# First attention stage: order of the floor rows' turn, of key low parts in halves, and of loads of queries, values, weight pieces and x

## What is computed

```python
ifg = jnp.concatenate([q, k, v], axis=-1)          # q = layernorm(x), k = v = ctx
ig = (ifg @ igate_w.T + igate_b).T
fg = (ifg @ fgate_w.T + fgate_b).T
log_f = jax.nn.log_sigmoid(fg)
cs = jnp.cumsum(log_f, axis=1)
log_D = where(mask, cs[:, :, None] - cs[:, None, :], -inf) + ig[:, None, :]
max_log_D = jnp.max(log_D, axis=-1, keepdims=True)
D_mat = jnp.exp(log_D - max_log_D)
C = jnp.einsum('hsd,htd->hst', qh, kh) / np.sqrt(DH) * D_mat
normalizer = jnp.maximum(jnp.abs(C.sum(axis=-1, keepdims=True)), jnp.exp(-max_log_D))
h = jnp.einsum('hst,htd->hsd', C / (normalizer + EPS), vh)
x = x + (h - mu) / jnp.sqrt(var + LN_EPS) * ln_scale
```

## Time and profile before

| | |
|---|---|
| median of 3 runs | 562.37 us (560.95 to 563.0) |
| the profiled execution | 565.76 us |
| its span, first to last instruction | 564.0 us |
| mean granted TensorE clock | 0.992 |
| TensorE matmul busy | 542.1 us, 96% |
| TensorE weight load busy | 455.0 us, 81% |
| VectorE busy | 324.3 us, 58% |
| ScalarE busy | 236.1 us, 42% |
| GpSimd busy | 72.7 us, 13% |

### The profile page before, as it was taken

One profiled execution on the slowest core, in us unless ns is written; L12 is line 12 of the kernel. 1 busy time (PEld: TensorE's weight loads), 2 busy tenths in 40 slices (PEclk: granted clock), 3 DMA queues, 4 the chain that ended last, 5 costly groups with the idle time before them and its releaser, 6 DMA issues.

```text
span 564.0 us, 8422 instructions
## 1 busy us (share of the span) xinstructions
PE 542.1 (96%) x2773; PEld 455.0 (81%) x2773; DVE 324.3 (58%) x792; ACT 236.1 (42%) x440; POOL 72.7 (13%) x107
## 2 busy tenths in 40 slices
PE   6899898999999999899999999999999999999996
PEld 5687687888988888778888878889788889788886
DVE  6568879868777698763434552443543543633333
ACT  6435546648798742561122351122441122531111
POOL 6233424203311432000000000000000000000000
PEclk9999899999999999999999999999999999999999
DMA  6684616273959676100000100000000000000001
GB/s 178 186 230 116 179 46 203 56 257 123 403 193 281 247 241 213 46 1 1 0 1 0 38 2 1 0 1 19 20 0 1 1 1 29 9 1 0 1 0 40
DMA packets 29860, 47.44 MB, mean 84 GB/s; under 512 B 3392, under 2 KB 21184, under 8 KB 29440
## 3 DMA queue, kind: packets, MB, share of 16 engines
q1 hardware_dynamic: 24848, 30.14, 16.8%
q0 software_dynamic: 4848, 16.78, 9.2%
q10 hardware_dynamic: 128, 0.05, 0.0%
HBM read 40.27 MB, written 2.10 MB: 75 GB/s over the span
## 4 chain that ended last, share of the span: by engine, by line
PE 58%; issue 8%; POOL 2%; DVE 1%; POOLq 0%; ACT 0%; DVEq 0%; ACTq 0%
PE ps L942 57%; POOL rstd L453 1%; POOL h L564 1%; PE ps L598 0%; PE ps L906 0%; DVE qr L1577 0%; DVE x L1565 0%; DVE xn L1326 0%; DVE h L1624 0%; DVE alT L1604 0%; ACT silD L1272 0%; DVE xT L1333 0%; POOL w L553 0%; POOLq L564 0%; POOL w L555 0%
## 5 line engine op out<-in xcount | busy, mean ns | idle before, releaser
L1289 ACT ACTIVATE h<-ps,scol 128x512 f32<-128x512 f32 x64 | 44.1, 690 | 175.3 <-PE ps L942 175.2
L942 PE MATMUL ps<-hBt,h 128*128 128x512 f32 x512 | 117.5, 390 | 0.0
L942 PE MATMUL ps<-hA,h 128*128 128x512 f32 x512 | 117.3, 390 | 0.0
L942 PEld LDWEIGHTS ps<-hA,h 128*128 128x128 f32 x512 | 95.9, 188 | 20.4 <-DVE hA L1631 0.6
L942 PEld LDWEIGHTS ps<-hBt,h 128*128 128x128 f32 x512 | 95.8, 188 | 20.3 <-DVE hBt L1631 0.6
L942 PE MATMUL ps<-xT,w 128*128 128x512 f32 x256 | 61.8, 396 | 1.3 <-DVE xT L1333 1.0
L942 PEld LDWEIGHTS ps<-xT,w 128*128 128x128 f32 x256 | 46.4, 188 | 15.2 <-issue 5.9
L1649 DVE CAST hBt<-h 128x512 fp32r<-128x512 f32 x32 | 13.7, 427 | 73.7 <-ACT h L1289 73.7
L1649 DVE CAST hA<-h 128x512 fp32r<-128x512 f32 x32 | 13.7, 427 | 70.0 <-ACT h L1289 70.0
L453 POOL TENSOR_TENSOR rstd<-ve,mhalf 128x4 f32<-128x4 f32 x16 | 16.4, 1024 | 262.9 <-DVE ve L1321 262.9
L1272 ACT ACTIVATE silD<-ps,scol 128x512 f32<-128x512 f32 x32 | 22.0, 689 | 45.6 <-PE ps L942 45.6
(11 more groups left out here) (176 smaller groups left out, 885.0 us busy)
## 6 DMA issues: line engine op xcount, KB each, us to landing
looked<-w_all_in SPq DMA_DIRECT2D x16, 704.0 KB, 5.6
h<-w_all_in POOLq DMA_DIRECT2D x16, 512.0 KB, 6.8
V<-ctx_in SPq DMA_DIRECT2D x8, 512.0 KB, 4.5
Qb<-xT SPq DMA_DIRECT2D x64, 64.0 KB, 2.1
w<-w_all_in POOLq DMA_DIRECT2D x3, 1024.0 KB, 6.9
x<-x_in SPq DMA_DIRECT2D x4, 512.0 KB, 5.0
kstA<-ctxT_in SPq DMA_DIRECT2D x4, 512.0 KB, 4.7
kstC<-ctxT_in SPq DMA_DIRECT2D x4, 512.0 KB, 6.4
```

Source lines behind the costliest of these rows:

```text
L942: last = mm(o, a, b, start=(k == 0 and p == 0), stop=(k == n_k - 1 and p == 1))
L1289: fn(h32[:, m % 2, :], ps[:, 2 + m % 4, :], ACT.Gelu, scale=scol[:, L + 1, m:m + 1])\
```

## The change

- The loads of x of groups 3 and 4 are issued behind the startup constants instead of behind the first queries.
- In a group, SyncE issues the third sequence's queries, then the next keys, then the gate rows, then the last sequence's queries, and only then waits for the product with V and issues the next values, directly ahead of the z rows.
- The low part of the keys is made in two instructions of 512 columns with a counter for each; the gate matmuls wait for the first half and, one chunk later, for the second. The second attention keeps whole ones.
- GpSimd issues the weight pieces behind h_root of the first sequence and inv_root instead of ahead of them.
- TensorE turns the floor rows behind the last sequence's scores instead of before its exponents, and VectorE copies them behind the last two weighings instead of behind x's normalisation.

```diff
@@ sync
             sp.dma_start(diag[:, :], diag_in).then_inc(s["consts"], 16)
+            for g in range(2, G):
+                sp.dma_start(x[:, Q * g:Q * g + Q, :], x_in[Q * g:Q * g + Q].rearrange("b s d -> s b d"))\
+                    .then_inc(s["x_rest"], 16)
             sp.wait_ge(s["klo_done"], 1)
...
             queries_in(0, 0, 0)
-            for g in range(2, G):
-                sp.dma_start(x[:, Q * g:Q * g + Q, :], x_in[Q * g:Q * g + Q].rearrange("b s d -> s b d"))\
-                    .then_inc(s["x_rest"], 16)
...
+                    queries_in(g, u, 2)
                     with sp.If(i < 1):
 
                         sp.wait_ge(s["klo_done"], 2 + u)
                         sp.dma_start(kstA[:, :, :], ctxT_in[:, :, (2 + u) * GT:(3 + u) * GT])\
                             .then_inc(ctxT_ld[u], 16)
-                    queries_in(g, u, 2)
-                    def early():
+                    if u == 0:
                         gates_in(gn)
+                    else:
+                        with sp.If(i < 1):
+                            gates_in(gn)
+                    queries_in(g, u, 3)
+                    def following():
                         sp.wait_ge(s["pv_done"], Q * g + 2)
                         values(gn, 1 - u)
+                        lead_in(gn, 1 - u)
                     if u == 0:
-                        early()
+                        following()
                     else:
                         with sp.If(i < 1):
-                            early()
-                    queries_in(g, u, 3)
-                    if u == 0:
-                        lead_in(gn, 1 - u)
-                    else:
-                        with sp.If(i < 1):
-                            lead_in(gn, 1 - u)
+                            following()
@@ gpsimd
+            def k_lo_apart(n, u):
+
+                pool.wait_ge(s["khi_done"], n + 1)
+                for c, name in ((0, "klo_first"), (1, "klo_done")):
+                    nc.gpsimd.tensor_tensor(kT[:, u, 1, c, :], kstA[:, c, :], kT[:, u, 0, c, :], ALU.subtract)\
+                        .then_inc(s[name], 1)
...
                         with pool.If(i > 0):
-                            k_lo(G - 1, kstA[:, :, :], 1)
+                            k_lo_apart(G - 1, 1)
                             h_root(2 * Q - 1, 1)
                     else:
                         with pool.If(i < 1):
-                            k_lo(2, kstA[:, :, :], 0)
+                            k_lo_apart(2, 0)
                         h_root(Q * g - 1, 1)
+                    h_root(Q * g, 0)
+                    inv_root(g + 2)
                     if u == 0:
                         pool.wait_ge(s["gate_moved"], 32 * (g + 2))
                         pool.sem_inc(s["pieces_go"], 1)
...
                             pieces(1, 0)
-                    h_root(Q * g, 0)
-                    inv_root(g + 2)
@@ tensor
                     if c == KD:
+                        pe.wait_ge(s["klo_first"], g + 1)
+                    if c == KD + 1:
                         pe.wait_ge(s["klo_done"], g + 1)
...
-                        if q == Q - 1:
-                            more(lambda: turn_e(gn))
-                            if u == 1:
-                                if_later(pe, i, flag_total)
+                        if q == Q - 1 and u == 1:
+                            if_later(pe, i, flag_total)
                         for k in (2 * q, 2 * q + 1):
                             expo(g, u, k)
                         for k in (2 * q, 2 * q + 1):
                             qk(g, u, k)
+                        if q == Q - 1:
+                            more(lambda: turn_e(gn))
@@ vector
             def k_lo(n, par):
                 dve.wait_ge(s["khi_done"], n + 1)
-                v.tensor_tensor(kT[:, par, 1, :, :], kstA[:, :, :], kT[:, par, 0, :, :], ALU.subtract)\
-                    .then_inc(s["klo_done"], 1)
+                for c, name in ((0, "klo_first"), (1, "klo_done")):
+                    v.tensor_tensor(kT[:, par, 1, c, :], kstA[:, c, :], kT[:, par, 0, c, :], ALU.subtract)\
+                        .then_inc(s[name], 1)
...
                             x_norm(g + 2, (8, 12)[u] - 8 * i)
-                            more(lambda: floor_copy(gn, 1 - u))
                             head_norm(b - 2, q - 2)
                         if q == Q - 1:
+                            more(lambda: floor_copy(gn, 1 - u))
                             finish(b - 1, u, q - 1)
```

More of the change, by code:

```diff
@@ L235, in two_layers @@
             raw_here raw_seen hnm_ready hve_ready lns_ready gw_lo gw_cast const_set mv_ready rstd_ready xn_ready tr_done xhi_done xlo_done x_free
-            khi_done klo_done gate_done gate_copied gate_moved ab_ready ln_ready ncs_ready er_ready z_ready
+            khi_done klo_done klo_first gate_done gate_copied gate_moved ab_ready ln_ready ncs_ready er_ready z_ready
             z_moved er_turned et_ready expo_done d_ready qk_done c_ready pv_done pv_used hstat_ready hrs_ready
```

## The result

| | before | after |
|---|---|---|
| median | 562.2 us (560.09 to 566.24, 22 runs) | 566.35 us (563.13 to 570.3, 22 runs) |
| the profiled execution | 565.76 us | 565.2 us |
| its span | 564.0 us | 563.5 us |
| its mean granted TensorE clock | 0.992 | 0.997 |

The ratio of the times is 1.0057 with an interval of 1.0038 to 1.0077: the change makes the kernel 0.57% slower, some 3.2 us by this ratio (4.15 between the medians). The forecast was 2.4 us faster, and the range ended at 562.9.

What follows compares the result with a forecast made beforehand. TensorE was taken to bound the kernel, busy 322.8 of the last 328 us. Terms summed to -3.95 us, -2.35 with one clock fall, so 562.4 - 2.4 = 560.0 us; range 557.8 to 562.9.

Steps and rivals of the forecast that it cites:

- x sooner: At the start, z rows land at 24.6 us: 1.4 us gained, and 1.6 more if the clock holds.
- Turn of the floor rows: At each group's end, Er waits go and x's turn waits for VectorE's copy: +0.45, -1.6, +0.7 us in groups 1 to 3.
- Queries ahead of values: On SyncE's queue, the last sequence's queries land in 2.0 us instead of 4.5 to 4.8, but zero time is gained.
- Weight pieces later: Pieces beside the next group's z rows and first queries cost 0.3, 0 and 0.2 us in groups 1 to 3.
- upper bounds of 1.7, 0.4 and 1.7: Most that waits for the next group's first queries could cost beside the weight pieces, groups 1 to 3: 3.8 us in all.
- The rule of turns between queues: DMA engines go round robin between queues, so GpSimd's pieces slow SP's loads in any order: 3.8 us instead of 0.5.
- Halves: Key low parts in two instructions cut TensorE's wait from 0.63 to 0.1 us: 0.5 gained in groups 2 and 3 each.
- Clock falls: Idle time of some 2.0 us before x's turn in three groups halves the clock once, costing 1.6 us.
- (d): Rival, chance 0.07: slower, weight pieces delay first queries at the first score block of groups 2 to 4; 563.3 us at full price.

Runs made afterwards that it cites:

- pieces put back: The after kernel with GpSimd's weight pieces put back ahead of h_root and inv_root, everything else kept: 560.31 us, ratio 0.9941.
- `lows` later: The after kernel with GpSimd's subtraction `lows` moved behind the second sequence's h_root: 566.08 us, ratio 1.0023.
- copy put back: The after kernel with VectorE's floor copy put back behind x's normalisation, TensorE's turn of the floor rows left late: 566.9 us, ratio 1.0078.
- turn undone: The after kernel with floor copy and weight pieces put back, and TensorE's turn of the floor rows again ahead of the last exponents: 558.97 us, ratio 0.9894.
- both put back: The after kernel with both VectorE's floor copy and GpSimd's weight pieces put back where before had them: 558.08 us, ratio 0.9898.

## Why the prediction was wrong, step by step

*x sooner* (-1.4, -1.6): right. Forecast 24.6 for the first z matmul, found 24.20 after 0.34 us of waiting, and clock 1.00 at 26 to 28 us. The first product with V came 3.4 us sooner, against 3.0. Over the runs it brought only 1.9, by the version with x alone: the fall that it avoids is in the trace of before, but not in every execution (see the end of this section).

*Turn of the floor rows* (+0.45, -1.6, +0.7): its mechanism was right. No Er is left; in its place stands the wait before the turn of x, 2.74, 1.57 and 2.44 us where 2.0 were forecast, 2.05 and 2.05; VectorE shows no gap before its last two weighings. The 0.45 lost in group 1 is borne out where nothing else disturbs it: with the pieces put back x is turned 12.45 us behind the first product with V (31.07 to 43.52), and 11.95 in before (34.59 to 46.54). The excess of 0.9 and 0.65 in groups 1 and 3 is `x_norm` (2.29 and 2.03 for 1.38), and no term of the sum had it. I had costed what moves on GpSimd's queue by its issues and roots and not by `lows`, which is moved too and reads two inputs beside VectorE. The experiment with `lows` later shows the cause. The Trainium skill (SBUF — State Buffer, Who interferes with whom) says that VectorE and GpSimd share one pair of ports, and that a `tensor_scalar` may be of a kind that takes it, so that the second to come waits. The rows agree roughly in size: 0.9 us more beside a subtraction of 0.75, and 0.65 more beside one of 0.78.

*Queries ahead of values* ("zero for all of it"): wrong. The landing times came nearly as forecast (2.0 us for the last sequence's; 5.2, 3.1 and 4.8 for the next group's first, forecast 4 or more), but undoing this order costs 3.5 us. I read 0.66, 0.85 and 0 of waiting for queries in before and took them for the whole lateness. TensorE came to them late because of Er. The gain of the turn that I booked as -1.6 rests on this edit: without it the turn alone measures 1.0019, and turn and copy together 1.0075.

*Weight pieces later* (+0.3, 0, +0.2): this is the term that failed. With the pieces put back, the stretches from the first product with V to the first scores of groups 2, 3 and 4 take 14.29, 23.51 and 23.64 us. In after they take 16.68, 23.81 and 25.49: 4.5 us more in all, where 0.5 was booked, and some 6 over the runs. In these 4.5 are the longer `x_norm` (0.9 and 0.65) and the fall (1.4); in group 1 they leave hardly anything for the z rows and queries, which land while TensorE waits for the copy. The traffic by itself is seen in the version with `lows` later: 2.0, -0.3 and 1.95 us. That is the upper bounds of 1.7, 0.4 and 1.7, and a little above them in groups 1 and 3; I had chosen values near the lower ones. Where the copy is out of the way as well, the z rows alone are waited for by 2.44, 1.22 and 2.94 us (copy put back), against 1.50, 0 and 0 with the pieces put back too.

Three things in it were wrong. I reasoned from bytes (1.8 MB at 343 GB/s end at 48.3), as if it were enough that the bulk ends before the queries are wanted. The end itself was put too early: 48.3 is 44.9 in after, whose start is 3.4 us ahead, but the last piece, issued at 40.08, lands 6.3 us later, at 46.4, and 39.6 to 47.6 us carries 2.15 MB, the second sequence's queries with it. And the small transfers end with the bulk, not at their share: in copy put back the pieces issued at 39.16 and 39.70 land at 44.6 and 46.5, and the z row issued at 39.20 is waited for until 45.9. Last, I asked only when the first queries are wanted. The z rows are wanted before them (44.89 against 45.36 with the pieces put back), and in before they were issued ahead of the queries, at 41.0 to 43.6, just where the pieces' issues were put; in front of that TensorE was already waiting for the copy. The rule of turns between queues (the Trainium skill, DMA: Bandwidth & Descriptors, in its part on queues, rings and completion order) that I set beside the row, and then weighed lower than the bytes, is borne out by the 2.0 and 1.95 us.

*Halves* (-0.5, -0.5): the durations are right (2.53 for two, 1.27 each, forecast 1.28), the wait for low parts is gone, and the time is unmoved by it: 0.9897 against 0.9898. A gain of up to 0.5% is not excluded by the intervals.

*Clock falls*: one of three forecast, one in the trace, behind the longest idle time of 2.74 us, at 1.4 us by the first score (forecast 0 to 1.6). The idle times of 1.79, 1.57 and 1.79 us with the pieces put back showed none in the profiled execution, and the others' mean clocks (0.998 to 1.0) leave room for one short one at most. So the number in the profiled execution was right and the number over runs was not: after's mean clock is 0.994 (0.988 to 1.0), that of the 34 runs of before 0.996. The stretched `x_norm` and the late z rows push idle times from 1.8 us to 2.4 and more.

By groups of after's trace: group 1 from its first product with V lost 2.9, of it 1.4 to 1.6 the fall, 0.9 `x_norm`, and the forecast 0.45; group 2 gained 1.7 against 2.1; group 3 lost 2.3 against 0.4, of it 0.65 `x_norm` and 1.05 z rows. Of the rivals, (d) came true in its mechanism, at the z rows as well as at the queries, and at about its full price of 3.8 us by the traffic alone (2.0 + 1.95); `x_norm` and the falls come on top. It had 0.07 because I argued that "the traffic ends before".

One more step failed ahead of all these. The median of before was set against a profiled execution with two falls in it, and the gain from avoiding the first was counted in full; the 1.6 of group 2 holds the second. Runs of before at full clock (560.5) cannot have them to give: the three fastest runs with x sooner alone, at 0.997 to 0.999, took 559.31 to 559.76, some 1 us less and not 3. That such executions lack the fall need not come from z rows that land sooner. The version with only TensorE's turn moved has the startup of before, and its profiled execution waits 1.94 us for the z rows, until 25.98, where before waits 1.93, until 26.05; yet its clock stays at 1.00 from 24 to 34 us, and the first product with V starts at 32.92 and not at 34.59. It holds at 1.00 behind an idle time of 2.57 us too. So the length of an idle time did not decide alone in these traces, and a forecast that counts falls from one execution takes its luck for the rule. What makes executions of one program differ in this stays open.

## What to carry to other kernels

Before a bulk load is moved, list the small transfers that are issued in the 5 us around its new place and when each is wanted: here those of 16 and 64 KB landed 5 to 7 us after their issue, with the bulk and not at their share of the bytes. When a wait is taken away, look for the one beneath it by the issue and landing times of what comes next, not by the wait's own row, which shows only what the earlier one left over. An edit of many parts is best taken apart on the chip: here x sooner, the queries' new order and the halves gave 1.1% together (the version with the turn undone), and the move of two roots ahead of the pieces took 1.2 to 1.8% away.

## What the runs showed of the hardware that was not expected

- A 16 KB transfer issued from SyncE at 39.20 us, beside four of 384 KB that GpSimd issued at 38.0 to 39.7 us, was waited for until 45.9 (copy put back), 6.7 us; the 384 KB issued at 39.16 and 39.70 us took 5.4 and 6.8. With the last of them issued 3.2 us ahead of it and not 0.5 us behind it (both put back) it was still 5.1 us.
- A two-input subtraction on GpSimd (0.75 us) made VectorE's four `tensor_scalar` of 128x256 f32 take 2.29 us in place of 1.37. GpSimd's DMA issues in the same stretch did not.
- Executions of one program differ by some 5 us along with the mean granted clock: before took 559 to 562 us at 0.999 or 1.0, and 565.4 to 566.6 at 0.992. A single profiled execution stands for one of them only.
- The same idle time is followed by half speed in one execution and not in another: behind 1.93 us the clock was 0.53 at 26 to 28 us (before), behind 1.94 us at the same place of the program it was 1.00 (turn of the floor rows alone), and behind 2.44 us 1.00 (after, group 3).
